# A decoder layer on one core: the causal mask of the cross-attention added by TensorE instead of VectorE

## The reference

```python
x = _layernorm(x + _L0_attn_ref(x, ...))           # windowed attention, 17 offsets, 16 heads
x = _layernorm(x + _L0_xattn_ref(x, ctx, ctx))     # causal attention against ctx, one head of 256
x = _layernorm(x + _L0_ffn_ref(x, ...))            # 8 experts of 1024, the best 2 of each token

def _L0_xattn_ref(query, key, value):
    scores = jnp.einsum('bqd,bkd->bqk', query, key)
    tri = jnp.triu(jnp.ones((L, L), dtype=scores.dtype), k=1) * MASK_VAL    # 1e10
    scores = scores - tri[None, :, :]
    probs = jax.nn.softmax(scores / SCALE, axis=-1)                         # SCALE = 16
    return jnp.einsum('bqk,bkd->bqd', probs, value)
```

## Time and profile before

| | |
|---|---|
| runs | 1216.67 us median of 3 (1216.6 to 1220.08) |
| profiled execution | 1216.64 us, span 1214.6 us, mean granted clock of TensorE 0.907 |
| busy over the span | TensorE 955.6 us (79%), VectorE 846.3 (70%), GpSimd 741.0 (61%), ScalarE 439.4 (36%) |
| cross-attention, 541 to 698 us | TensorE 120.96 us, VectorE 119.08, ScalarE 82.85, GpSimd 8.05, granted clock 0.92 |
| one sequence, 614.4 to 632.9 us | 18.50 us: TensorE 14.28 us, VectorE 15.32, ScalarE 10.59, GpSimd 1.01, granted clock 1.00 |
| chain that ended last, by line | L746 17%, L754 11%, L1366 7%, L756 5%, L1116 5%, L674 2%, L648 1% |

### The profile page before, as it was taken

How to read it: one execution, slowest core, us unless ns; L and a number is a source line. 1 busy time by engine, 2 the same in 40 slices (tenths; PEclk the granted TensorE clock), 3 DMA queues, 4 the chain that set the end, 5 groups by cost and what they waited for, 6 DMA issues and landing times.

```text
span 1214.6 us, 24812 instructions
## 1 busy us (share of the span) xinstructions
PE 955.6 (79%) x8007; PEld 770.2 (63%) x8008; DVE 846.3 (70%) x1296; ACT 439.4 (36%) x959; POOL 741.0 (61%) x531
## 2 busy tenths in 40 slices
PE   7983189878887887758788527999999999999940
PEld 4541178777876877746566426777777777777730
DVE  5899999998998998516888793444444444444435
ACT  3675233333333333415555422222222222323315
POOL 3564789999999999710000026666666666666522
PEclk9997598998999998869999768999999999999985
DMA  3361102112121111257667221222222232222236
GB/s 99 81 120 39 39 26 62 53 55 64 44 65 43 65 65 43 86 223 259 221 207 264 104 74 46 45 46 43 46 43 44 43 47 44 44 43 43 30 67 232
DMA packets 70136, 100.46 MB, mean 83 GB/s; under 512 B 9312, under 2 KB 51872, under 8 KB 69152
## 3 DMA queue, kind: packets, MB, share of 16 engines
q1 hardware_dynamic: 52816, 76.86, 20.4%
q0 software_dynamic: 16128, 18.93, 9.8%
q10 hardware_dynamic: 1152, 4.19, 0.8%
HBM read 73.96 MB, written 26.38 MB: 83 GB/s over the span
## 4 chain that ended last, share of the span: by engine, by line
PE 44%; DVE 21%; issue 16%; POOL 11%; DMA 4%; ACT 3%; DVEq 0%; SPq 0%; POOLq 0%; ACTq 0%
PE psum L746 17%; PE psum L754 11%; DVE mid L1366 7%; PE psum L756 5%; POOL mid L1116 5%; PE psum L674 2%; PE psum L617 2%; PE psum L597 2%; PE psum L738 2%; DVE arena L1513 1%; ACT arena L1044 1%; PE psum L648 1%; PE psum L600 1%; DMA sum_dram<-arena,mid 1%; DMA out<-arena 1%
## 5 line engine op out<-in xcount | busy, mean ns | idle before, releaser
L617 PE MATMUL psum<-consts,mid 128*128 128x128 f32 x2176 | 279.4, 295 | 85.9 <-POOL mid L1116 85.9
L617 PEld LDWEIGHTS psum<-consts,mid 128*128 128x128 f32 x2176 | 274.3, 210 | 97.3 <-issue 52.1
L746 PE MATMUL psum<-arena 128*128 128x128 f16 x3456 | 290.8, 220 | 4.0 <-issue 3.6
L746 PEld LDWEIGHTS psum<-arena 128*128 x3456 | 242.7, 98 | 75.9 <-issue 8.8
L1116 POOL TENSOR_TENSOR mid<-arena 128x2304 f32<-128x2304 f32 (+1 forms) x62 | 240.6, 3902 | 11.3 <-POOL arena L1108 7.9
L754 PE MATMUL psum<-arena 128*128 x576 | 218.1, 380 | 5.0 <-DVE arena L1665 1.2
L1207 POOL DMA_INDIRECT sum_dram<-arena,mid x72 | 142.8, 1983 | 45.2 <-issue 24.1
L1674 DVE SCALAR_TENSOR_TENSOR arena<-psum,arena 128x256 f32<-128x256 f32 x72 | 34.8, 484 | 189.7 <-ACT arena L1016 163.6
L756 PE MATMUL psum<-arena 128*128 x576 | 157.0, 273 | 0.0
L1366 DVE TENSOR_TENSOR mid<-psum,arena 128x4352 f32<-128x4352 f32 x32 | 149.7, 4678 | 1.0 <-issue 0.7
L1373 DVE TENSOR_REDUCE psum<-mid 128x272 f32<-128x4352 f32 x32 | 150.0, 4686 | 0.0
(11 more groups left out here) (196 smaller groups left out, 1410.3 us busy)
## 6 DMA issues: line engine op xcount, KB each, us to landing
arena<-w_t SPq DMA_DIRECT2D x64, 256.0 KB, 2.9
arena<-w_t SPq DMA_DIRECT2D x16, 1024.0 KB, 10.3
arena<-x SPq DMA_DIRECT2D x32, 128.0 KB, 2.1
arena<-x_dram SPq DMA_DIRECT2D x8, 512.0 KB, 5.0
arena<-ctx_t SPq DMA_DIRECT2D x8, 512.0 KB, 5.9
arena<-ctx SPq DMA_DIRECT2D x8, 512.0 KB, 6.4
x_dram<-mid SPq DMA_DIRECT2D x8, 512.0 KB, 3.3
arena<-sum_dram SPq DMA_DIRECT2D x8, 512.0 KB, 4.9
```

The source lines that it names most:

```text
L617: last = nc.tensor.matmul(psum[:, u, c * P:(c + 1) * P], products[half][:, w, c * P:(c + 1) * P], ident, start=(a + w == 0 and c == 0), st ...
L746: last = nc.tensor.matmul(dst, block_of(w, e, 0, c * F + j * P, P), x[:, u, c * P:(c + 1) * P], start=(k == 0 and c == 0), stop=(k == 2 an ...
```

## The change

VectorE's four additions a sequence (`mask`) and the semaphore `masked` go. TensorE accumulates a third product onto each tile's diagonal block: the identity as stationary operand, the mask as moving one. `find_peak(t)` waits for `s_done` itself.

```diff
@@ TensorE, attend
                     for c in range(C):
-                        last = nc.tensor.matmul(psum[:, t, 0:(t + 1) * P], x1_t[:, c, t * P:(t + 1) * P],
-                                                ctx_ts[:, u, c, 0:(t + 1) * P], start=(c == 0), stop=(c == C - 1))
-                    last.then_inc(s_done, 1)
+                        nc.tensor.matmul(psum[:, t, 0:(t + 1) * P], x1_t[:, c, t * P:(t + 1) * P],
+                                         ctx_ts[:, u, c, 0:(t + 1) * P], start=(c == 0), stop=False, skip_group_check=True)
+                    nc.tensor.matmul(psum[:, t, t * P:(t + 1) * P], ident, consts[:, AT_MASK:AT_MASK + P], start=False,
+                                     stop=True, skip_group_check=True).then_inc(s_done, 1)
@@ VectorE, attend
-                def mask(t):
+                def find_peak(t):
                     dve.wait_ge(s_done, QT * b + t + 1)
-                    diag = psum[:, t, t * P:(t + 1) * P]
-                    nc.vector.tensor_tensor(diag, diag, consts[:, AT_MASK:AT_MASK + P], ALU.add).then_inc(masked, 1)
-
-                def find_peak(t):
-                    dve.wait_ge(masked, QT * b + t + 1)
                     nc.vector.tensor_reduce(top_peak[:, u, t:t + 1], psum[:, t, 0:(t + 1) * P], op=ALU.max,
                                             axis=AX.X).then_inc(peak_found2, 1)
...
-                mask(0)
-                mask(1)
                 if past(b, 1):
                     norm2(b - 1, 1 - u)
                 find_peak(0)
                 find_peak(1)
-                mask(2)
                 scale_peaks(0)
                 if past(b, 2):
                     low_part(b - 2, 1)
-                mask(3)
                 find_peak(2)
                 find_peak(3)
```

More of the change, by code:

```diff
@@ L402, in decoder_layer @@
         peak_ready = sem("peak_ready")
-        masked = sem("masked")
         peak_found2 = sem("peak_found2")
```

## The result

| | before | after |
|---|---|---|
| median of 6 runs | 1217.31 us (1215.1 to 1220.08) | 1222.8 us (1219.69 to 1225.1) |
| ratio | | 1.0043, 95% interval 1.0026 to 1.0060 |
| profiled execution | 1216.64 us, span 1214.6 | 1219.69 us, span 1217.6 |

What follows compares the result with a forecast made beforehand. The bound was taken to be L1525, the copy of the logits, where VectorE and TensorE arrive nearly together. Terms 0.44 + 0.63 + 0.17 = +1.24 us on 1216.64 gave 1217.9 us, range 1215.3 to 1220.5.

Steps and rivals of the forecast that it cites:

- What bounds the stage, and the place L1525: VectorE's copy of the router's logits, where VectorE and TensorE arrive nearly together; TensorE's slack 0.11 us in sequence 4.
- The price of a product, 0.21 us: Each added 128-column f32 product on TensorE is two records at the pace of L617, 0.21 us.
- The rule weighed in the prediction: On TensorE, weight loads overlap matmuls only across row groups, so each added record would pay load and stream serially.
- What leaves VectorE, 0.28 us: Without the four additions VectorE alone reaches L1525 0.28 us sooner: third addition 0.08, fourth 0.20, first two nothing.
- VectorE's busy time, -9.4 us: Dropping 32 additions of 0.295 us lowers VectorE's busy time by 9.4 us.
- Sequence by sequence, +1.07 us in 1 to 7: L697's delay of 0.21 us less its slack at L1525: 0.44 us in sequences 2 to 5, 0.63 in 1, 6, 7.
- Sequence 0, +0.17: Eight added records cost 0.86 us at the first scores, less 0.69 saved on VectorE: net +0.17 us.
- The clock falls elsewhere: Rival: a shifted half-clock stretch reaches the last L674s or vanishes, 1 to 2 us either way; over 2 us, chance 0.03.
- free products: Rival: the added products cost TensorE nothing, 1.09 us gained in all, so 1215.6 us; chance 0.12.
- VectorE's whole time: Rival: all 9.4 us of VectorE's additions come off the end, 1207.2 us; chance 0.03.
- Loads that set the pace: Rival: TensorE's weight loads set 0.38 us a product, 5.3 us more, 1222 us; chance 0.10 for paced or serial loads.
- Serial loads: Rival: each added TensorE record also pays its load, 0.59 us a product, about 1228.7 us; chance 0.10 with paced loads.

Runs made afterwards that it cites:

- after_late: The changed kernel with VectorE's second weight splitting of a sequence moved behind the updates of tiles 0 and 1: 1209.12 us, ratio 0.9930 to the kernel before.
- before_late: The kernel before, additions kept, with VectorE's second weight splitting of a sequence moved behind the updates of tiles 0 and 1: 1208.15 us, ratio 0.9923.
- no_mask: The changed kernel without TensorE's mask products, so neither products nor additions: 1214.76 us, ratio 1.0007 to the kernel before.
- products_and_adds: The kernel before with TensorE's four mask products added and VectorE's four additions kept: 1223.43 us, ratio 1.0066.
- fourth_on_dve: The changed kernel with products for tiles 0 to 2 only and tile 3's mask added on VectorE: 1216.04 us, ratio 1.0000 to the kernel before.
- masks_early: The changed kernel with the four products issued one sequence ahead, in TensorE's idle stretch, scores accumulating onto them: 1216.36 us, ratio 1.0008 to the kernel before.
- before_delayed: The kernel before with three small VectorE copies added ahead of the second weight splitting in sequences 1 to 7, no product: 1220.06 us, ratio 1.0023.
- after_filled: The changed kernel with four unused identity products more in TensorE's idle stretch, sequences 0 to 6: 1219.55 us, ratio 1.0024 to the kernel before.

## Why the prediction was wrong

- **What bounds the stage, and the place L1525:** right. After, L1516 waits for L697 in every sequence, and the fourth product alone, put back on VectorE, returns the time to 1.0000.
- **The price of a product, 0.21 us:** right, 0.22 in the trace. One reading behind it is loose: 68 records in 7.86 us are 0.116 each, and 0.113 only if the tail of the last one is left out, so that row gives 0.23 a product as it stands; it changes nothing. The rule weighed in the prediction, of loads that cannot lie under streams, fails here too: six records ahead of the transposes are still hidden.
- **What leaves VectorE, 0.28 us:** 0.19. The fourth addition gave its 0.20. The third did let the scaling start 0.09 us sooner (L1475 at 617.53 - 615.59 = 1.94 behind L1510, before 616.38 - 614.35 = 2.03), but from L1510 to the long L1504 it is 617.95 - 615.59 = 2.36 us, and before 616.70 - 614.35 = 2.35: an issue gap of 0.25 us ahead of L1504, 0.16 before, took it back. The wait for L697 covers this, so the sequence is as forecast. Counted as in the prediction, from the moment at which VectorE could have started the copy (0.08 us behind the start of L1475, 621.48), that wait is 0.30 us, not 0.38; the 0.21 of the row leaves out the overlap.
- **VectorE's busy time, -9.4 us:** -6.1, for the overlap of neighbours that the prediction had itself used for the fourth addition.
- **Sequence by sequence, +1.07 us in 1 to 7:** right in the sequences without a fall (0.08 to 0.29 each), and 0.9 us in all where the row is broken (after_late against before_late, intervals overlapping).
- **Sequence 0, +0.17:** too small in places. From the first scores to the first copy it was 23.62 us before, and 23.92, 24.31, 24.46 and 24.52 in the four profiles of after: 0.3 to 0.9 more, of which 0.21 is sequence 1's. The clock rises at another point of the scores each time: 4.0 us behind their start in the kernel before, 3.8, 4.6, 4.9 and 5.0 in after, in the order of the times above.
- **The failed step:** "The clock falls elsewhere", priced at "1 to 2 us either way" with a chance of 0.03 for more, "This widens the range, not the forecast". The place it named, the last L674s at half clock, is the place where the time went. What it had wrong is the count: it treated a fall as a single event that might shift. In the changed kernel a fall repeats: it lengthens its sequence from 18.6 to 20.3 us or more, the next fall is 20.5 us away, and two to four sequences in a row pay 1.7 to 1.9 us each: 3.9 us in the profile of after with the steady cost in it, and four times in two others. Of the 5.5 us between the medians about 1.2 are the sum; that the remaining 4.3 are falls is an estimate from these profiles, two or three falls of 1.7 to 1.9 us.
- **The rivals:** free products (1215.6) and VectorE's whole time (1207.2) are out by no_mask at 1.0007. Loads that set the pace (1222) gave the right size for the wrong reason: a product took 0.22 us and not 0.38, and TensorE doubled the length of some records by its clock. Serial loads (1228.7) are out by the same row. In the chances, 0.82, 0.13 and 0.04 add up to 0.99.

Still open: what makes the first fall land at the costly place. Where no fall shortens it, TensorE's wait ahead of the last products is 1.74 to 1.85 us in the kernel before, which has no such row in its profile, and 1.86 to 2.19 after; but no_mask had 1.84 and 1.96 without a row. All profiles of after and of products_and_adds have the first costly fall at the same sequence, 2. fourth_on_dve shows that the product ahead of L697 is needed, and masks_early that products elsewhere don't bring the row; no run delays L697 without a product, and none shows what ends a row.

## What to carry to other kernels

Moving work from a waiting engine to another is worth only the slack of the second at the next join: here 0.15 us or less, read from two rows. Put such work where its engine idles (a sequence earlier here, where it cost nothing that could be measured), or leave it. Where TensorE waits in every round of a loop, as it did here for some 1.9 us, two questions belong to the price of a clock fall. Does it land where a wait covers it, or in work that the others wait for? And is the round, lengthened by a fall, about as long as the distance to the next one (here 20.3 to 20.6 and 20.5 us)? Then a slower case belongs in the sum, with a fall in several rounds and not in one.

## What the runs showed of the hardware

- The low stretches of the granted clock inside the cross-attention lasted 3.4 us (6.8 twice in before_delayed). In rounds of 20.3 to 20.6 us they came 20.5 us apart; elsewhere the distance was longer, 37.5 us in after_filled and 54.6 in the kernel before.
- A fall that began 1.1 to 2.1 us behind the copy of the logits was covered by TensorE's wait for VectorE in the kernel before, the change, no_mask and fourth_on_dve. One that began 5.5 to 6.8 us behind it, in the change and in products_and_adds, made its sequence 1.7 to 1.9 us longer. The same early fall cost 0.6 us in masks_early and some 1.5 in before_late, where that wait was shorter or gone.
- The best version was not the change: the kernel before with one instruction of VectorE moved behind two updates, 0.9923 of its time, 9 us.
